# Six shifted-attention layers: values in rows of 32, TensorE's products regrouped by array shape, its stream written out

## The reference, cut to what matters

```python
def look(t):                      # windows of 32 tokens, and the window before
    p = jnp.pad(t, ((0, 0), (0, 0), (1, 0), (0, 0), (0, 0)))
    return jnp.concatenate([p[:, :, :nw], p[:, :, 1:]], axis=3)
...
q = l2norm(q) * qs
k = l2norm(k) * ksc
q = q * cos * scale + rotate_half(q) * sin * scale
k = k * cos * inv + rotate_half(k) * sin * inv
sim = jnp.einsum('bhwie,bhwje->bhwij', bq, bk2) * QK_SCALE
attn = jax.nn.softmax(jnp.where(mask, -big, sim), -1)
out = jnp.einsum('bhwij,bhwje->bhwie', attn, bv2)
...
# per layer, on tokens of which half the features are shifted by one:
x = attn_layer(shift_tokens(x), Wqkv, qs, ksc, Wo) + x
x = ffn_layer(shift_tokens(x), g, bln, W1, b1, W2, b2) + x   # layer norm, exact gelu gate
```

## Time and profile before

| | |
|---|---|
| median of 3 runs | 4655.95 us (4654.68 to 4657.93) |
| the profiled execution's own time | 4656.79 us |
| its span, first to last instruction | 4655.0 us |
| granted TensorE clock, mean over the span | 0.935 |
| PE busy | 4112.3 us (88%) |
| DVE busy | 3561.9 us (77%) |
| ACT busy | 2988.6 us (64%) |
| POOL busy | 2212.4 us (48%) |

### The profile page before, as it was taken

The page is one execution under the profiler, slowest core; times in us unless marked ns, Lnnn a source line. Parts: engine busy times, 40 slices in busy tenths (PEclk is TensorE's granted clock), DMA queues, the critical chain, the costliest instruction groups (busy, mean ns, idle before and its releaser), DMA issues. The chain is left out here.

```text
span 4655.0 us, 112822 instructions
## 1 busy us (share of the span) xinstructions
PE 4112.3 (88%) x40172; PEld 2362.1 (51%) x40175; DVE 3561.9 (77%) x8496; ACT 2988.6 (64%) x5496; POOL 2212.4 (48%) x1392
## 2 busy tenths in 40 slices
PE   8969999999999999999999999999999953747635
PEld 5644555555555555555555555555555532635533
DVE  7878888888888888888888888888888846356441
ACT  3427777777777777777777777777777745645302
POOL 0006665665656656566566656656565500140006
PEclk9989999999999999999999999999999975868557
DMA  1013222322223222232222322223222200000202
GB/s 41 1 54 67 62 58 62 80 59 61 60 60 81 63 59 60 58 82 65 59 59 60 76 65 63 57 64 75 64 60 61 58 17 12 1 1 6 82 9 35
DMA packets 187828, 246.44 MB, mean 53 GB/s; under 512 B 88677, under 2 KB 129383, under 8 KB 187367
## 3 DMA queue, kind: packets, MB, share of 16 engines
q1 hardware_dynamic: 182054, 240.47, 22.2%
q0 software_dynamic: 5632, 4.33, 0.7%
HBM read 41.65 MB, written 14.30 MB: 12 GB/s over the span
## 5 line engine op out<-in xcount | busy, mean ns | idle before, releaser
L1234 POOL TENSOR_TENSOR f_rot_a<-f_rot_a,f_norm 128x1024 f32<-128x1024 f32 x384 | 730.4, 1902 | 996.1 <-DVE f_norm L1073 963.6
L1226 POOL TENSOR_TENSOR f_rot_a<-f_rot_a,f_rot_b 128x1024 f32<-128x1024 f32 x384 | 908.5, 2366 | 246.3 <-issue 213.6
L832 PE MATMUL f_bank<-f_w_vo,f_xs_t 128*64 128x512 f32 x3072 | 828.5, 617 | 24.5 <-ACT f_vo L1303 24.5
L1303 ACT ACTIVATE f_vo<-f_bank 128x512 f32<-128x512 f32 x768 | 457.0, 595 | 395.9 <-PE f_bank L832 385.9
L1294 ACT ACTIVATE f_squares<-f_bank 128x512 f32<-128x512 f32 x768 | 456.4, 594 | 295.5 <-PE f_bank L819 215.6
L1052 DVE TENSOR_TENSOR f_rot_a<-f_bank,f_rot 128x512 f32<-128x512 f32 x768 | 525.0, 684 | 83.4 <-DVE f_stat L1101 42.3
L1055 DVE TENSOR_TENSOR f_rot_b<-f_bank,f_rot 128x512 f32<-128x512 f32 x768 | 516.8, 673 | 0.0
L864 PEld LDWEIGHTS f_bank<-f_k_t,f_q_t 128*32 128x32 f32 x12288 | 313.6, 109 | 315.4 <-issue 162.4
L1059 DVE TENSOR_REDUCE f_sums<-f_squares 128x16 f32<-128x1024 f32 x384 | 464.9, 1211 | 1.6
L1315 ACT ACTIVATE f_k_t<-f_bank 64x512 f32<-64x512 f32 x768 | 449.2, 585 | 4.8 <-PE f_bank L854 0.3
L1240 POOL TENSOR_TENSOR f_prob<-f_score,f_stat 128x512 f32<-128x512 f32 x384 | 400.4, 1043 | 98.6 <-DVE f_stat L1105 98.6
(11 more groups left out here) (445 smaller groups left out, 7235.4 us busy)
## 6 DMA issues: line engine op xcount, KB each, us to landing
f_vo_off<-f_vo SPq DMA_DIRECT2D x1152, 128.0 KB, 2.3
f_vo_off<-f_vo SPq DMA_DIRECT2D x384, 64.0 KB, 2.0
f_w_qk<-in_Wqk SPq DMA_DIRECT2D x12, 512.0 KB, 5.9
f_vo_dram<-f_vo_pair SPq DMA_DIRECT2D x48, 128.0 KB, 1.8
f_x_shifted<-s_all SPq DMA_DIRECT2D x48, 128.0 KB
f_x_shifted<-s_all SPq DMA_DIRECT2D x48, 127.0 KB
f_w_vo<-f_vo_dram SPq DMA_DIRECT2D x10, 512.0 KB, 4.0
e_w<-in_e_W SPq DMA_DIRECT2D x2, 2048.0 KB, 12.1
```

The costliest lines, as they stand in the source:

```text
L832: done = nc.tensor.matmul(bank[V][64 * n:64 * n + 64, :], x, w_vo[:, 4 * g:4 * g + 4, n, :], start=True, stop=True)
L1226: nc.gpsimd.tensor_tensor(rot_a[:, slot, :, :], rot_a[:, slot, :, :], rot_b[:, g, :, :], ALU.add).then_inc(rot_summed, 1)
L1234: nc.gpsimd.tensor_tensor(heads, heads, over(norm[:, 16 * g:16 * g + 16], [128, 16, HEAD_DIM]), ALU.mult).then_inc(qk_normed, 1)
L1303: nc.scalar.activation(vo[:, g, 2 * (t % 2) + j, :], flat(V), ACT.Copy).then_inc((va_copied, vb_copied)[j], 1)
```

## The change

Values in rows of 32: the two matmuls of 64 columns in `values` become four of 32 columns; the output is the same. On TensorE, the order of a round is changed so that `values_a`, `scores`, `mix`, `values_b` follow each other twice in a round, and all products of full width stand between these two runs. The other engines' orders follow: on DVE `total(r-2, 1)` stands after both rotations of the next round, `highest(r-1, 0)` ahead of the rotation of k, `highest(r-1, 1)` behind that of q; on POOL `weigh` goes ahead of `scale`; on ACT the first exponential stands ahead of `copy_q` in every round (before, behind it in round 3), and the second one, with `seed(1)`, ahead of `copy_values(1, 1)` and `copy_q(1)`. On SP, `shift_x` goes between the two `shift_values` of round 2. TensorE's `body` is written out for all 51 passes; `Steady` marks a number for which every piece of the pass is there.

```diff
@@ stream order of SP
                         shift_values(p, r - 1, 0)
+                    if r == 2 and (q > 0 or not first):
+                        shift_x(p - 1, (q - 1) % PASSES)
+                    if r > 0 or q > 0 or not first:
                         shift_values(p, r - 1, 1)
...
-                    if r == 2 and (q > 0 or not first):
-                        shift_x(p - 1, (q - 1) % PASSES)
@@ values
-                for n in range(2):
-                    done = nc.tensor.matmul(bank[V][64 * n:64 * n + 64, :], x, w_vo[:, 4 * g:4 * g + 4, n, :], start=True, stop=True)
+                for w in range(4):
+                    at = 32 * (w % 2)
+                    done = nc.tensor.matmul(bank[V][32 * w:32 * w + 32, :], x[:, at:at + 32], w_vo[:, 4 * g:4 * g + 4, w // 2, :], start=True, stop=True)
@@ TensorE's body
-                        values_a(p, r - 1, 1)
                         turn_q(p, r - 1, 0)
...
                         turn_k(p, r - 1, 0)
-                        values_b(p, r - 1, 1)
...
                     if on(r - 1):
+                        values_a(p, r - 1, 1)
                         scores(p, r - 1, 0)
+                    if on(r - 2):
+                        mix(p, r - 2, 0)
+                    if on(r - 1):
+                        values_b(p, r - 1, 1)
                         turn_q(p, r - 1, 1)
...
-                    if on(r - 2):
-                        mix(p, r - 2, 0)
                     if on(r):
                         values_a(p, r, 0)
+                    if on(r - 2):
+                        mix(p, r - 2, 1)
                     if on(r - 1):
                         scores(p, r - 1, 1)
                     if on(r):
                         values_b(p, r, 0)
-                    if on(r - 2):
-                        mix(p, r - 2, 1)
-            stream(pe, body)
+            for p in range(LAST + 3):
+                body(Steady(p) if 3 <= p < LAST else p)
@@ DVE's body
-                    if r < 3 and on(r - 2):
-                        invert(1)
-                    if on(r):
                         rotate(p, r, 0, 1, 1)
-                    if r == 3 and on(r - 2):
+                    if on(r - 2):
                         total(p, r - 2, 1)
                         invert(1)
...
-                        rotate(p, r, 1, 1, 0)
                     if on(r - 1):
                         highest(p, r - 1, 0)
+                    if on(r):
+                        rotate(p, r, 1, 1, 0)
...
+                    if on(r - 1):
+                        total(p, r - 1, 0)
+                        invert(0)
                     if on(r):
                         length(p, r, 1)
                         inverse_lengths(p, r)
-                    if on(r - 1):
-                        total(p, r - 1, 0)
-                        invert(0)
...
-                    if on(r - 1):
-                        highest(p, r - 1, 1)
                     if on(r):
                         rotate(p, r, 1, 0, 0)
                         rotate(p, r, 1, 0, 1)
+                    if on(r - 1):
+                        highest(p, r - 1, 1)
...
-                    if r != 2 and on(r - 1):
-                        total(p, r - 1, 1)
@@ POOL's body
                         add_up(p, r, 0)
-                        scale(p, r, 0)
                     if on(r - 1):
                         weigh(p, r - 1, 0)
                     if on(r):
+                        scale(p, r, 0)
                         add_up(p, r, 1)
@@ ACT's body
-                    if r < 3 and on(r - 2):
+                    if on(r - 2):
                         exponential(p, r - 2, 1)
                     if on(r - 1):
-                        copy_values(p, r - 1, 1, 0)
                         copy_q(p, r - 1, 0)
-                    if r == 3 and on(r - 2):
-                        exponential(p, r - 2, 1)
...
-                        copy_values(p, r - 1, 1, 1)
...
                     if on(r - 1):
+                        copy_values(p, r - 1, 1, 0)
+                        exponential(p, r - 1, 0)
+                        seed(p, r - 1, 1)
+                        copy_values(p, r - 1, 1, 1)
                         copy_q(p, r - 1, 1)
                     if on(r):
                         square(p, r, 1, 0)
-                    if on(r - 1):
-                        exponential(p, r - 1, 0)
-                        copy_k(p, r - 1, 1)
-                        seed(p, r - 1, 1)
                     if on(r - 2):
                         copy_prob(p, r - 2, 1)
+                    if on(r - 1):
+                        copy_k(p, r - 1, 1)
```

More of the change, by code:

```diff
@@ L469, in _, with __add__, __sub__ @@
                     prob_copy(i - 2)
+class Steady(int):
+    def __add__(self, n):
+        return Steady(int(self) + n)
+    def __sub__(self, n):
+        return Steady(int(self) - n)
 def shifted_layers(nc, x_all, ident, ident_bf, dram):
@@ L585, in live @@
         def live(p, t):
-            return not isinstance(p, int) or 0 <= p * PASS_TILES + t < LAST * PASS_TILES
+            return not isinstance(p, int) or isinstance(p, Steady) or 0 <= p * PASS_TILES + t < LAST * PASS_TILES
         def has(p, back):
-            return not isinstance(p, int) or 0 <= p - back < LAST
+            return not isinstance(p, int) or isinstance(p, Steady) or 0 <= p - back < LAST
         def moved(p, t):
```

## The result

The changed kernel takes 4727.46 us (median of 4 runs, 4720.72 to 4733.39) against 4655.70 for the kernel before in the same comparison (4654.68 to 4657.93): a ratio of 1.0153, 95% interval 1.0135 to 1.0171. It is 1.5% slower, where 4622 us was forecast. The profiled execution took 4723.33 us, its span is 4721.5, and the granted TensorE clock over the span is 0.921 for 0.935.

What follows compares the result with a forecast made beforehand. TensorE was taken to set the pace at 70.72 us a pass; 4.5 us of work and 2.3 of old waits off, 6.2 of new waits on, gave 70.1. Gains of 28 and about 6 us made 4622 us, range 4500 to 4700.

Steps and rivals of the forecast that it cites:

- TensorE's work: Fewer shape changes on TensorE, 12 to 4 a round, save 1.13 us a round, 4.5 a pass.
- item 3: Round 3: exponential and its table load stand ahead of `copy_q(0)`, so `turn_k(0)` waits 2.9 us, the largest wait.
- the walk: All engines' new orders followed through a pass's four rounds: 15.9 + 18.4 + 16.9 + 18.9 = 70.1 us.
- Cost nothing: SP in round 2: `shift_values(1, 1)` queued behind the earlier `shift_x` starts about 1 us late, priced at nothing.
- item 4: Round 2: `take_gate` and exponential ahead of `copy_q(0)`, 0.3 us; round 0: `fold` behind the last `hide`, 0.35 us.
- Rival C: Slower: shape boundaries inside narrow runs keep 0.11 us each, 1.8 us a pass, 71.9, 4706 us; chance 0.07.
- The fetch: TensorE's 51 written-out bodies: some 300 more instruction packets, cost nothing, hidden; at most 1.9 us a pass, 80 in all.
- `shift_x` sooner: SP, round 2: DVE's 2.5 us wait for shifted x goes; cost nothing, gain only where DVE sets the pace.
- Item 1: All rounds: scores, `highest`, exponential, `seed(1)`, copies on ACT delay `turn_k(1)`; wait 0.35 us each, 1.4 a pass.
- Items 1 and 2: Round 1: score chain 0.35 us at `turn_k(1)`, plus 1.1 from `normalise` delaying `highest(0)`, and 0.1 for the seed.
- rival B: Faster: waits overlap more than walked; at 3 us of waits a pass 66.9, 4479 us; with none 4350; chance 0.24.
- D: Slower: chain behind the scores longer; 0.15 us more a round eats the gain, 0.4 more makes 4700 us; chance 0.15.

Runs made afterwards that it cites:

- the filled wait: Changed kernel with three groups of values computed again in round 3, between `project_q` and `turn_k`, where TensorE waits; 4680.53 us, ratio 1.0044 to the kernel before.
- all four edits: Changed kernel with round 3's exponential behind `seed(0)`, `seed(1)` behind `copy_q(1)` and a square, `w_qk`'s first half sent sooner, VectorE written out; 4537.96 us, ratio 0.9754.

## Why the prediction was wrong

The sign was wrong, and 4727 lies outside 4500 to 4700. What failed is no term of TensorE's work. It is item 3 of the walk, which gave the wait of round 3 its own length as its whole price and the clock behind it nothing. The steady pass was forecast at 70.1 and takes 72.24 on the mean, 2.14 us more, 94 us in passes 3 to 46. These come in three parts:

1. **The clock behind the wait of round 3: 56 to 60 us, shown** by the filled wait. Item 3 of the walk sized that wait rightly, 2.9 forecast and 3.0 measured, and left out what follows it. The prediction's last sentence named this as a thing that would make it wrong; it got no price and no chance. In the pass shown above it costs 1.7 us (0.42, 0.85 and 0.39 on the three steps behind the wait), the whole of 72.37 for 70.74. The Trainium skill, TensorE: Matmul & The Clock Gate, HAM oscillation, describes the like in another kernel, where a wait in every turn of a loop leaves the next products to start at the lower clock. The trace agrees, with 35 stretches in 44 passes. It should have been a rival on the slower side.
2. **The end of a layer: about 11 us, shown** by sending `w_qk` sooner. "Cost nothing" for SP's queue looked at one reader only, `mix`. The load of the next layer's `w_qk` stands behind the same `shift_values`, was 6.5 us early, and is 3.6 us early now, which is too late.
3. **Round 0: 28 us.** A pass at full clock takes 70.74, 0.64 over the walk. Round by round: 16.87 for 15.9, 18.19 for 18.4, 16.76 for 16.9, 18.92 for 18.9. All of the excess is in round 0: 0.71 at `project_k(1)` behind VectorE's loop turn, which the walk didn't have, and 0.63 at `fold` for the 0.35 of item 4. The 0.93 us of idle time at the turn stood in the trace before, but the product that follows it came 2.2 us later into the pass there and never met it. Without the turn VectorE's wait is gone and about 40 us with it, in a neighbouring kernel.

The three make 95 to 99 us for 94; they were measured in neighbouring kernels, so no closer fit is to be asked. Outside these passes, passes 0 to 2 lost 0.5 us where a gain of 6 was forecast, the last pass and the emptying of the pipeline lost 8.6 where nothing was forecast, and the stages behind the layers gave 8 back. For the last two no run shows a cause.

**TensorE's work: right.** A run takes 3.60 for 3.64, a group 0.88; with values in 64 columns the pass is 0.75 us longer. Rival C had the inner boundaries keep a part of their price: a group of 0.88 leaves at most 0.02 over a full-width projection's 0.86. PE's busy time fell by 3.5 us a pass.

**The fetch: right for what was asked, and blind to what was done.** The stream written out costs nothing (0.9998), with 293 packets more where some 300 were forecast. But the comparison was with a loop, and the loop would not have stayed as it was: with values in rows of 32 its body is fetched anew in each pass, and the kernel takes 4875 us. The written-out stream is what makes rows of 32 possible, some 143 us that stood in my sum as nothing. The Trainium skill, Runtime: NRT & Kernel Launch, Instruction fetch mechanics, says that a taken branch out of the fetched window stalls; the 2.50 us at the edge agree with it for the larger body, and no such stall shows for the smaller.

**`shift_x` sooner: wrong.** I gave it nothing. In the old place it costs some 290 us in the new order, measured with the exponential back and `w_qk` sooner. I priced the move against the old trace, where the wait was 2.5, and not against the new order, in which what stands ahead of it on SP is later.

**The walk.** Item 1, the chain behind the scores: 0.24 for 0.35 in each of rounds 0, 2 and 3. It is a real chain, since taking `seed(1)` out of it gives 57 us. Items 1 and 2 in round 1, the chain and `normalise`: 1.45 forecast at `turn_k(1)` and 1.15 measured, 0.1 forecast for the seed and 0.23 measured, round 18.2 for 18.4. Item 3: 3.0 for 2.9. Item 4: 0.21 for 0.3. So rival B, waits that melt, was wrong for this order, and so was D, a longer chain of item 1: the loss came elsewhere. Of the marks that the prediction set for itself, the wait of 2 to 3 us for `copy_q`, the short ones in other rounds, `values` as 128*32 and the queue's packets are all there; so is the fall of the granted clock. The waits that were walked come to 6.0 us a pass where 6.2 were forecast; VectorE's turn in round 0 comes on top.

**What the change could have been.** With the exponential of round 3 in its old place, the same change is at 0.998 of the kernel before, with all four edits at 0.975.

## What to carry to other kernels

A wait of TensorE can have two prices, its own length and the clock behind it: when a walk finds a single long wait in each turn, give the lower clock a rival of its own with a price and a chance (here 1.7 us behind 34 of 44 waits), and try splitting or filling the wait. When an engine's order moves something later, go through every instruction behind it in every queue that waits for it, loads of the next stage too, and price a moved step in the new order, not in the old trace. Before a looped body grows, look in the profile whether it is still fetched only once. And when an engine gets faster, look at the idle times of the others that it used to arrive too late to meet, a loop's turn among them.

## What the runs showed of the hardware that wasn't expected

- The granted clock fell to 1.2 GHz behind single idle times of 2.85 us in an otherwise dense stream (65.6 us busy of 70.7), 34 of 44 times: at 725.66 to 729.54 us the same wait left it at 1.00. Waits of 2.54 us were followed by it 10 of 44 times, waits of 3.1 to 4.7 at another place 29 of 44 times. Two waits of 1.1 and 1.4 us a few us apart were not followed by it in any steady pass.
- TensorE's looped body of 751 matmuls and 751 loads a pass is not fetched again (59 packets in the whole run, none in passes 4 to 43); with 64 more of each it is (457 packets, nine a pass), with 2.4 to 4.9 us of idle at a turn, about 3% of the time in both kernels that had it. Written out, the fetching of a pass cost no time that shows (0.9998).
- VectorE stands for 0.8 to 0.9 us at the turn of its hardware loop. It stood in the kernel before as well and cost TensorE nothing there; it counts when what comes right behind it is waited for: some 40 us here.
- The change of the array's shape costs 0.13 us a narrow group (1.01 against 0.88). Between groups of the same shape at most 0.02 shows, with all 128 rows in use and new weights in each.
